# A Mamba and expert layer on one core: jobs of the first chunk moved up by one slot, and the second block of y read ahead of the SiLUs

## What is computed

```python
xn = _rmsnorm(_layernorm(x), rms_w)
xs, res = jnp.split(xn @ W_in, 2, axis=-1)                 # 512 channels each
xs = jax.nn.silu(causal_conv(xs, conv_w) + conv_b)
dt, Bm, Cm = jnp.split(xs @ W_x, [512, 512 + 16], axis=-1)
dt = jax.nn.softplus(dt @ W_dt)
h_t = exp(A * dt_t) * h_(t-1) + dt_t * Bm_t * xs_t         # 16 states for each channel
y_t = sum over states of h_t * Cm_t
x = x + layernorm(x) + (y * jax.nn.silu(res)) @ W_out
x = x + (silu(z @ w1[e]) * (z @ w3[e])) @ w2[e]            # z = layernorm(x), e = token // 512
```

## Time and profile before

| | us |
|---|---|
| median of 3 runs | 1073.26 |
| lowest and highest | 1070.85, 1075.76 |
| the profiled execution | 1073.56 |
| its span, first to last instruction | 1071.8 |
| busy in it: DVE, PE, POOL, ACT | 951.7, 942.2, 891.6, 679.8 |
| TensorE clock, mean granted | 0.958 of full |

### The profile page before, as it was taken

One profiled execution on the slowest core, in us unless ns is written; L12 is line 12 of the kernel. 1 busy time (PEld: TensorE's weight loads), 2 busy tenths in 40 slices (PEclk: granted clock), 3 DMA queues, 4 the chain that ended last, 5 costly groups with the idle time before them and its releaser, 6 DMA issues.

```text
span 1071.8 us, 12989 instructions
## 1 busy us (share of the span) xinstructions
PE 942.2 (88%) x4160; PEld 600.2 (56%) x4160; DVE 951.7 (89%) x1039; ACT 679.8 (63%) x1146; POOL 891.6 (83%) x491
## 2 busy tenths in 40 slices
PE   5978698999998989989999889989999897668879
PEld 4545455655665456645655556645656555655655
DVE  5797789999998899998998999998999989998941
ACT  4665666676667866676667766676667765667410
POOL 1597699898998889897998979988998979998810
PEclk9999898999999999999999999999999999769889
DMA  4570045012721038011641029010661027100010
GB/s 161 239 277 20 11 184 201 1 62 92 267 116 48 14 145 329 1 62 55 246 174 39 23 94 369 11 62 11 228 236 39 3 94 276 66 20 29 27 47 20
DMA packets 42852, 117.86 MB, mean 110 GB/s; under 512 B 8608, under 2 KB 27040, under 8 KB 32672
## 3 DMA queue, kind: packets, MB, share of 16 engines
q1 hardware_dynamic: 40928, 116.99, 29.3%
q10 hardware_dynamic: 1856, 0.04, 0.1%
HBM read 110.21 MB, written 6.82 MB: 109 GB/s over the span
## 4 chain that ended last, share of the span: by engine, by line
DVE 34%; PE 29%; ACT 16%; issue 16%; POOL 3%; DMA 0%; DVEq 0%; POOLq 0%; ACTq 0%
DVE ring L658 23%; PE gbank L1001 21%; DVE ring L643 9%; PE ybank L1053 6%; ACT ebank L784 4%; POOL ring L493 2%; ACT hb L941 1%; ACT sres L848 1%; POOL hc L507 1%; ACT xs L844 1%; DVE dt_ L623 1%; ACT xin L925 1%; ACT L849 1%; ACT x L894 1%; ACT L840 1%
## 5 line engine op out<-in xcount | busy, mean ns | idle before, releaser
L507 POOL TENSOR_TENSOR hc<-ring,c_all 128x1024 f32<-128x1024 f32 x255 | 599.0, 2366 | 102.0 <-DVE ring L658 72.0
L658 DVE TENSOR_TENSOR_SCAN ring<-ebank,state,ring 128x512 f32<-128x512 f32 x512 | 625.1, 1269 | 61.7 <-ACT ebank L784 46.4
L784 ACT ACTIVATE ebank<-dt_,a_neg 128x512 f32<-128x512 f32 x512 | 348.9, 688 | 261.6 <-DVE ring L658 259.1
L1053 PEld LDWEIGHTS ybank<-ident,hc 128*128 128x128 f32 x2048 | 243.7, 146 | 161.7 <-issue 76.0
L1053 PE MATMUL ybank<-ident,hc 128*128 128x128 f32 x2048 | 274.4, 283 | 66.0 <-ACT yt L864 50.1
L493 POOL TENSOR_TENSOR ring<-b_all,u 128x1024 f32<-128x1024 f32 x95 | 224.8, 2366 | 0.0
L643 DVE TENSOR_TENSOR ring<-b_all,ubank 128x1024 f32<-128x1024 f32 x159 | 190.3, 1197 | 0.0
L1001 PE MATMUL gbank<-xT,w 128*128 128x512 f32 x320 | 158.1, 634 | 29.8 <-ACT xT L803 17.3
L1001 PE MATMUL gbank<-xT,w_a 128*128 128x512 f32 x256 | 119.6, 611 | 10.1 <-DVE dt_ L623 6.4
L1001 PEld LDWEIGHTS gbank<-xT,w 128*128 128x128 f32 x320 | 60.3, 201 | 93.6 <-issue 78.6
L1001 PE MATMUL gbank<-xs,w_a 128*128 128x512 f32 x224 | 100.8, 593 | 0.0
(11 more groups left out here) (128 smaller groups left out, 746.7 us busy)
## 6 DMA issues: line engine op xcount, KB each, us to landing
b_all<-bc_kept SPq DMA_DIRECT2D x32, 1024.0 KB, 7.1
c_all<-bc_kept SPq DMA_DIRECT2D x32, 1024.0 KB, 8.4
w<-in_L_ffn_w_dram SPq DMA_DIRECT2D x16, 640.0 KB, 4.7
w_a<-wc_kept SPq DMA_DIRECT2D x7, 1024.0 KB, 4.8
w_a<-win_kept SPq DMA_DIRECT2D x6, 1024.0 KB, 6.6
w2s<-in_L_ffn_w_dram SPq DMA_DIRECT2D x8, 640.0 KB, 5.2
xin<-in_L_attn_x_dram SPq DMA_DIRECT2D x9, 512.0 KB, 3.6
x<-in_L_attn_x_dram SPq DMA_DIRECT2D x7, 512.0 KB, 6.4
```

What stands on the lines that cost most here:

```text
L507: ch_ok.by(e.tensor_tensor(hc[:, q % HC, :, :], ring[:, q % RING, :, :], c_all[:, n:n + NG, :], ALU.mult))
L658: h_ok.by(e.tensor_tensor_scan(row, ebank[j % 2][:, :], row, initial=state[:, q, n:n + 1], op0=ALU.mult, op1=ALU.add))
L784: e_ok.by(e.activation(ebank[j % 2][:, :], dt_[:, d, :], ACT.Exp, scale=a_neg[:, d, k:k + 1]))
L1053: last = e.matmul(ybank[:, cols(b)], hc[:, q % HC, n, cols(b)], ident[:, :], is_transpose=True, start=(k == 0 and n == 0 and b == 0), stop ...
```

## The change

Only the tables of the first chunk are touched. No instruction is added or taken away. The late blocks 2 and 3 of dt are passed through softplus (ScalarE), read (VectorE) and multiplied into u (GpSimd) one slot sooner. The jobs of ScalarE and VectorE for the next chunk stand one slot sooner (XT, IN, CV, the SiLU stretch, RES, BC, DT 0 to 2), while TensorE's own slots stay, but for BC, YT 1 and DT 0 to 2, which are one slot sooner. `y_read(1)`, which was at slot 21, behind the SiLU stretch and a pair of exponentials, is now at slot 19, right ahead of the SiLU stretch, which itself went from slot 20 to 19. `res(2, 3)` of the late part and `y_read(0)` go from slot 12 to 11. `normal` goes one slot later, from 28 to 29. `x_stats` on VectorE stays at slot 20 but now stands behind `gated(0)`. The last numbers in `FIRST` only say how long a bank counts as taken; each product gets the same bank as before, with the same product ahead of it.

```diff
-            (0, "late", "DT", 1, 4.2), (1, "late", "WC", 2, 4.9), (4, "late", "DT", 2, 8.2), (6, "late", "DT", 3, 10.2),
+            (0, "late", "DT", 1, 4.2), (1, "late", "WC", 2, 4.9), (4, "late", "DT", 2, 7.2), (6, "late", "DT", 3, 9.2),
...
-            (19, "front", "RES", 2, 22.2), (19, "front", "RES", 3, 22.4), (22, "front", "BC", 0, 24.4), (22, "scan", "YT", 1, 24.2),
-            (23, "front", "DT", 0, 26.2), (25, "front", "DT", 1, 28.2), (26, "front", "DT", 2, 30.2), (27, "front", "DT", 3, 32.4),
+            (19, "front", "RES", 2, 21.2), (19, "front", "RES", 3, 21.4), (21, "front", "BC", 0, 23.4), (21, "scan", "YT", 1, 23.2),
+            (22, "front", "DT", 0, 25.2), (24, "front", "DT", 1, 27.2), (25, "front", "DT", 2, 29.2), (27, "front", "DT", 3, 32.4),
...
-            table0 = [(5, "late", u_of(1)), (9, "late", u_of(2)), (11, "late", u_of(3)), (21, "handed", hand_on),
-                      (22, "next", front), (27, "front", u_of(0)), (29, "front", u_of(1)), (31, "front", u_of(2))]
+            table0 = [(5, "late", u_of(1)), (8, "late", u_of(2)), (10, "late", u_of(3)), (21, "handed", hand_on),
+                      (22, "next", front), (26, "front", u_of(0)), (28, "front", u_of(1)), (30, "front", u_of(2))]
...
-            table0 = [(0, "late", fed), (4, "late", dt_of(1)), (8, "late", dt_of(2)), (10, "late", dt_of(3)), (16, "front", convolved(0)),
-                      (17, "front", convolved(1)), (18, "front", convolved(2)), (19, "front", convolved(3)), (20, "next", x_stats),
-                      (21, "scan", gated(0)), (24, "scan", gated(1)), (26, "front", dt_of(0)), (28, "front", dt_of(1)),
-                      (30, "front", dt_of(2)), (30, "scan", gated(2)), (31, "front", dt_of(ND - 1))]
+            table0 = [(0, "late", fed), (4, "late", dt_of(1)), (7, "late", dt_of(2)), (9, "late", dt_of(3)), (15, "front", convolved(0)),
+                      (16, "front", convolved(1)), (17, "front", convolved(2)), (18, "front", convolved(3)), (20, "scan", gated(0)),
+                      (20, "next", x_stats), (23, "scan", gated(1)), (25, "front", dt_of(0)), (27, "front", dt_of(1)),
+                      (29, "front", dt_of(2)), (30, "scan", gated(2)), (31, "front", dt_of(ND - 1))]
...
-                      (4, "late", wc_rest(2)), (7, "late", softplus(2)), (9, "late", softplus(3)), (10, "late", res(0, 1)),
-                      (12, "late", res(2, 3)), (12, "scan", y_read(0)), (13, "late x", turned("XT")), (14, "front", before_conv(0, 1)),
-                      (15, "front", before_conv(2, 3)), (20, "scan", silus), (21, "front", res(0, 1)), (21, "scan", y_read(1)),
-                      (22, "front", res(2, 3)), (24, "front", bc_read), (25, "front", softplus(0)), (27, "front", softplus(1)),
-                      (27, "scan", y_read(2)), (28, "next", normal), (29, "front", softplus(2)), (30, "front", softplus(ND - 1)),
+                      (4, "late", wc_rest(2)), (6, "late", softplus(2)), (8, "late", softplus(3)), (10, "late", res(0, 1)),
+                      (11, "late", res(2, 3)), (11, "scan", y_read(0)), (12, "late x", turned("XT")), (13, "front", before_conv(0, 1)),
+                      (14, "front", before_conv(2, 3)), (19, "scan", y_read(1)), (19, "scan", silus), (20, "front", res(0, 1)),
+                      (21, "front", res(2, 3)), (23, "front", bc_read), (24, "front", softplus(0)), (26, "front", softplus(1)),
+                      (27, "scan", y_read(2)), (28, "front", softplus(2)), (29, "next", normal), (30, "front", softplus(ND - 1)),
```

More of the change, by code:

```diff
@@ L129, in mamba_moe_layer @@
         FIRST = [
-            (0, "late", "DT", 1, 4.2), (1, "late", "WC", 2, 4.9), (4, "late", "DT", 2, 8.2), (6, "late", "DT", 3, 10.2),
+            (0, "late", "DT", 1, 4.2), (1, "late", "WC", 2, 4.9), (4, "late", "DT", 2, 7.2), (6, "late", "DT", 3, 9.2),
             (7, "late", "RES", 0, 10.7), (7, "late", "RES", 1, 10.8), (8, "late", "RES", 2, 11.6), (8, "late", "RES", 3, 11.7),
-            (9, "late x", "XT", 0, 13.8), (10, "front", "IN", 0, 14.2), (10, "front", "IN", 1, 14.4), (11, "front", "IN", 2, 15.2),
-            (11, "front", "IN", 3, 15.4), (12, "front", "CV", 0, 16.2), (13, "front", "CV", 1, 17.2), (14, "front", "CV", 2, 18.2),
-            (15, "front", "CV", 3, 19.2), (17, "scan", "YT", 0, 20.2), (18, "front", "RES", 0, 21.2), (18, "front", "RES", 1, 21.4),
-            (19, "front", "RES", 2, 22.2), (19, "front", "RES", 3, 22.4), (22, "front", "BC", 0, 24.4), (22, "scan", "YT", 1, 24.2),
-            (23, "front", "DT", 0, 26.2), (25, "front", "DT", 1, 28.2), (26, "front", "DT", 2, 30.2), (27, "front", "DT", 3, 32.4),
+            (9, "late x", "XT", 0, 12.8), (10, "front", "IN", 0, 13.2), (10, "front", "IN", 1, 13.4), (11, "front", "IN", 2, 14.2),
+            (11, "front", "IN", 3, 14.4), (12, "front", "CV", 0, 15.2), (13, "front", "CV", 1, 16.2), (14, "front", "CV", 2, 17.2),
+            (15, "front", "CV", 3, 18.2), (17, "scan", "YT", 0, 19.2), (18, "front", "RES", 0, 20.2), (18, "front", "RES", 1, 20.4),
+            (19, "front", "RES", 2, 21.2), (19, "front", "RES", 3, 21.4), (21, "front", "BC", 0, 23.4), (21, "scan", "YT", 1, 23.2),
+            (22, "front", "DT", 0, 25.2), (24, "front", "DT", 1, 27.2), (25, "front", "DT", 2, 29.2), (27, "front", "DT", 3, 32.4),
             (29, "scan", "YT", 2, 31.4), (30, "next", "XT", 0, 31.6)]
```

## The result

| | before | changed |
|---|---|---|
| median of 20 runs each, us | 1075.65 | 1065.64 |
| lowest and highest, us | 1070.85, 1078.84 | 1063.18, 1071.99 |
| the profiled execution, us | 1073.56 | 1067.03 |
| its span, us | 1071.8 | 1065.2 |

The ratio is 0.9915, with a 95% interval of 0.9899 to 0.9932: faster, by some 9 us (7.3 to 10.9) where 7.0 were forecast; the two medians of the table are 10.0 apart. The two profiled executions differ by only 6.6 in their spans. The points on the clock and the median, further down, say as much as is known of the difference.

What follows compares the result with a forecast made beforehand. Neither VectorE nor TensorE alone was the bound; a 43.7 us GpSimd chain ended chunk 0. Starting it at 128.5 instead of 135.48 saves 7.0: 1073.56 to 1066.56, given as 1066.5 because the profiled execution lay 0.3 above the median; range 1062.5 to 1072.5.

Steps and rivals of the forecast that it cites:

- Where the time goes: End of chunk 0: a 43.7 us GpSimd chain from slot 22's product; the gain is how much sooner it begins.
- The late reads of dt: Chunk 0, VectorE's read of dt 3 goes ahead of slot 10's scans; RES 3 and the sums follow 2.46 us sooner.
- The clock: TensorE's late RES 3 in chunk 0, after about 4.1 us idle: stays slow at 3.16 us; full speed would add 1.3.
- the third rival: RES 3 at full clock (1.3 us) and TensorE ahead in chunk 1: 1064 and below; chance 0.11.
- The stretch: SiLUs and y 1's copy, slots 17 to 21: slot 20 at 117.5, slot 21 at 122.4 against 123.15.
- the early part: Chunk 0 up to slot 17: dt reads and IN 2.46 us sooner, slot 17 at 101.3.
- The chain start: GpSimd's product of slot 22, chunk 0: starts at 128.5 instead of 135.48, 7.0 us sooner.
- The step that failed: SiLU stretch, chunk 0: moving it ends TensorE's 10.32 us stop, GpSimd's 7.38 wait and the 2.22 before slot 23.
- the second rival: Early part of chunk 0 brings nothing, slot 22 ends at 130.9: gain 4.6 us, time 1069; chance 0.18.
- what comes next late: After slot 20: RES 3 waits for gated(0) at 120.5, ends at 123.7; slot 25 at 137.4, 3.2 us slack.
- The second half: BC, DT and u one slot sooner at chunk 0's end: GpSimd's order changes, its sum doesn't; 7.0 us gain arrives.
- The clock's rival: TensorE stays at 1.2 GHz after a gap of some 8 us before RES 3: 1074, up to 1082; chance 0.06.

Runs made afterwards that it cites:

- the trace with the statistics covered: VectorE's x_stats moved from slot 20 to slot 19, into its wait for the SiLUs, against the changed kernel; ratio to before 0.9920.

## Why the prediction was right, point by point

**Where the time goes.** Chunk 0 ends in a chain on GpSimd that has no idle time. This was the best reading of the forecast: 43.7 us in every trace but one, whatever the kernel, and what an edit did to slot 3 of chunk 1 it did by moving the chain's start.

**The late reads of dt.** RES 3 was forecast 2.46 sooner and came 2.74 sooner (77.39 to 74.65), and 3.7 sooner in the trace with the statistics covered. The forecast left out the 0.53 that VectorE's slot 8 stood for exponentials behind softplus(2) and no longer does. Against it, a load of this trace landed 0.36 later, and GpSimd's first product with C, which waits for it, holds what follows; in the trace with the statistics covered that product started at 44.13, which is nearly all of the 1.0 by which its RES 3 comes ahead of the 74.65. The product before and after:

```profile
44.74 2.36 POOL L507 TENSOR_TENSOR hc<-ring,c_all 128x1024 f32<-128x1024 f32 x1 [10.96 <-DMA c_all<-bc_kept]
```

```profile
45.10 2.36 POOL L507 TENSOR_TENSOR hc<-ring,c_all 128x1024 f32<-128x1024 f32 x1 [11.16 <-DMA c_all<-bc_kept]
```

IN at 84.15 was 83.97.

**The clock.** RES 3 was left at its slow 3.16 and took 3.56, behind 3.76 of idle time. Such a product takes 1.88 at full clock and 3.78 when it is slowest, so the 3.16 was slow only in part. In the second trace of the changed kernel it took 1.99, behind 2.74: the faster RES 3 that the third rival priced at 1.3 does occur. What was not foreseen is that the pair of IN might run slow as well: 5.37. This cost the changed kernel's trace 1.7 between IN and slot 17 (102.83, forecast 101.3) and at the SiLU stretch, where the copy of y 1 started at 110.54 and not at 108.9.

**The stretch.** From the copy to slot 20 8.5 (forecast 8.6), slot 21 at 123.77 (122.4), all late by the same 1.4 to 1.6. It gives back on VectorE what the early part had gained, as said. Once `y_read(1)` and `gated(0)` have moved, the whole stretch a slot sooner gains nothing more: the kernel before with the two moves alone needs 43.44 from IN to the chain start, the changed kernel 44.20. With `y_read(1)` behind the SiLUs it gains 3.4 (45.45 against 48.87), since the stop for `yt` then ends sooner too, 34.6 behind the start of IN and not 38.6. That is why the read is worth so little within the changed kernel.

**The chain start.** 129.87 instead of 128.5, a gain of 5.6 instead of 7.0 in this pair of traces. With 3.67 for the pair of IN it would be 1.70 sooner, 128.17: a gain of 7.3, of which 2.6 come from the earlier IN and 4.7 from the stretch, where the forecast had 2.46 and 4.54. With the load of `c_all` landed as in the trace of before, the 0.36 above, it would be 7.7. This is an estimate from the traces; no trace of the changed kernel itself has that clock.

**The step that failed** is the reason, not the sum. The forecast put what the stretch buys to the read of y 1 (TensorE's 10.32, GpSimd's 7.38), and the second rival priced the stretch at 4.6 with nothing earlier. The read alone gives 0.9. The other 4.5 come only with `gated(0)`, which frees a bank for RES 3, and behind RES 3 stands the sum that GpSimd waits for; a bank free still sooner gives 2.4 more. The forecast had this path, under "what comes next late", but with almost no slack and at no price: RES 3 done at 123.7, and with a sum of 0.9 behind it at 124.6, just before slot 21 ends at 124.8. GpSimd's product of slot 21 started at 127.09, behind 3.17 of waiting for that sum, and was done at 129.4. With two steps of 0.2 behind it GpSimd was free at 129.87, and VectorE's slot 22 ended at 129.79: the two held the chain's start together. This is why covering the statistics on VectorE gave only 0.4.

**Luck.** The 1066.5 lies 0.9 from the measured 1065.64, closer than the working deserves. It was counted from a time of before of 1073.3, which came out at 1075.65, 2.4 higher, and the medians differ by 10.0 where 6.8 were forecast. The two misses cancel.

**The second half, and the rivals.** The new order of BC, DT and u was worth nothing, as said. From slot 3 of chunk 1 to the end of the span the traces of before have 892.6 and 892.8, those of the changed kernel 891.6 and 894.3. So the first pair of traces shows nothing given back, and the second 1.5. The forecast named a longer chunk 1 as a sign of being wrong, and it is longer: from its slot 3 to that of chunk 2 it takes 121.6 in both traces of before, 122.9 and 123.2 in those of the changed kernel. The change isn't the cause of most of it. Both lengths occur under both orders: 122.8 in the kernel before with `y_read(1)` moved, 121.6 in the changed kernel with it back. And a chunk of 121.2 comes later instead in the first trace of the changed kernel (chunk 3), but in none of its second. What makes such a chunk short stays open. The clock's rival didn't come: DT 0 took 3.60 at 132.66.

**The median.** It moved by more than the forecast and than the two spans. The runs of before lie in two groups: nine of the 20 at 1070.9 to 1073.9, nine at 1077.4 to 1078.8, and the median, 1075.65, falls between them, where there are only two runs. In the changed kernel 16 lie at 1063.2 to 1068.2 and four at 1070.8 to 1072.0. Median against median the lower groups are 7.8 apart and the upper 7.1, which is the size of the forecast and of the 7.3 to 7.7 above. The rest of the 9 to 10 is that the upper group has fewer runs. A trace of before from its upper group has its setup 3.6 later (46.75 against 43.16), and so has one of the changed kernel (46.77 against 43.31). In before the delay is still 3.8 at slot 3 of chunk 1 and 4.0 at the end. In the changed kernel it is 1.1 at slot 3, but 3.9 at the end: the two late traces are 6.7 apart in their spans, the two early ones 6.6. So it isn't shown that a late setup costs the changed kernel less. Whether the change makes late setups rarer isn't shown either: over all runs here the upper group has 29 of 68 for before and 7 of 26 for the changed kernel, which chance can do.

## What to carry to other kernels

When a wait is removed, look for the next resource that the same queue needs: here a stop of 10.32 us hid a wait for a PSUM bank, held until an instruction of 0.7 us on another engine. Removing the stop alone gave 0.9 us, and the bank 4.5 more; of the bank alone the trace of before promises nothing. A queue that runs without idle time up to where the bound engine waits for it is the thing to time: find its first instruction, and price each edit by how much sooner that one starts. A large wait that is certain, such as a table switch, is a place to put work that others wait for (the statistics, and above all what frees a bank), not only work that has to be done sometime.

## What the runs showed of the hardware

The same products at the same place ran at either level of TensorE's clock from run to run. The first pair of IN, behind 2.5 to 3.8 us of idle time, took 3.67 in seven traces (2.4 GHz) and 5.37 in seven (in part 1.2 GHz). The kernels whose order up to that place is the one of before are on both sides, and so are those with the changed order. Over 84 to 90 us the mean granted clock was 1.00 of full in the trace of before and 0.72 in that of the changed kernel. The setup did the same: the 48 records of the products of dt's weights took 7.29 in some traces and 8.79 to 9.04 in others, and in the second trace of before the products ahead of them (L1038) took 5.48 instead of 3.69. Over 39 to 46 us TensorE was busy all the time in both traces of before, with a mean granted clock of 1.00 in one and 0.60 in the other, and in the two pairs of traces of one and the same kernel what follows was 3.5 and 3.6 later. Each of these single events is as large as the edits that were measured, so two traces can't be compared in their spans alone. The marks in the middle do better: what lies between two of them was 18.61 twice in the changed kernel, 20.08 and 20.38 in the one before, and 43.74 to 43.79 over the chain in 13 of 14 traces.
